# Transfers of each pair parted eight and eight over two queues, one PSUM bank, one copy and the last batch's output shares moved

## The reference

```python
def _ffn(x, w1, b1, w2, b2):
    h = gelu(x @ w1 + b1, approximate=False)          # 256 -> 1024
    return h @ w2 + b2                                # 1024 -> 256
def _attn(x, w_qkv, w_out, b_out):
    q, k, v = heads(x @ w_qkv)                        # 16 heads of 64
    sim = (q * 64 ** -0.5) @ k.T - slope_h * abs(i - j)
    sim = where(causal, -max, sim)                    # only j <= i counts
    return merge(softmax(sim) @ v) @ w_out + b_out
x = x + 0.5 * _ffn(layernorm(x), ...)
x = x + _attn(layernorm(x), ...)
x = x + 0.5 * _ffn(layernorm(x), ...)
```

## Time and profile before

| | |
|---|---|
| median of the runs | 2169.64 us |
| profiled execution | 2169.53 us |
| its span | 2167.7 us |
| PE, PEld busy | 2115.9, 1715.6 us |
| DVE, ACT, POOL busy | 1525.4, 1272.0, 1143.1 us |
| granted PE clock, mean | 0.996 of full speed |
| spread transfers | SP 1392, POOL 646, ACT 10 |

### The profile page before, as it was taken

The page is one execution under the profiler, slowest core; times in us unless marked ns, Lnnn a source line. Parts: engine busy times, 40 slices in busy tenths (PEclk is TensorE's granted clock), DMA queues, the critical chain, the costliest instruction groups (busy, mean ns, idle before and its releaser), DMA issues.

```text
span 2167.7 us, 42138 instructions
## 1 busy us (share of the span) xinstructions
PE 2115.9 (98%) x14480; PEld 1715.6 (79%) x14480; DVE 1525.4 (70%) x4121; ACT 1272.0 (59%) x3156; POOL 1143.1 (53%) x1988
## 2 busy tenths in 40 slices
PE   7999999999999999999999999999999999999998
PEld 6687787877878788787886878878787787877867
DVE  6776767767676676767767677676766777667674
ACT  5756656466565665756557465674646646565572
POOL 2754636546474563745547365473654637445361
PEclk9999999999999999999999999999999999999999
DMA  3432515234152342524425143251533415234142
GB/s 132 132 84 81 144 32 144 78 94 122 45 142 69 107 109 54 145 56 117 108 62 139 45 136 90 69 149 28 145 83 94 128 40 146 69 103 113 45 132 59
DMA packets 130294, 209.70 MB, mean 97 GB/s; under 512 B 42192, under 2 KB 70960, under 8 KB 130080
## 3 DMA queue, kind: packets, MB, share of 16 engines
q1 hardware_dynamic: 97888, 143.86, 23.6%
q0 software_dynamic: 25952, 58.38, 10.7%
q10 hardware_dynamic: 6240, 4.76, 0.8%
HBM read 14.95 MB, written 8.39 MB: 11 GB/s over the span
## 4 chain that ended last, share of the span: by engine, by line
PE 57%; DVE 19%; ACT 8%; issue 6%; POOL 4%; ACTq 3%; SPq 1%; DMA 1%; POOLq 0%; DVEq 0%
PE ps L361 56%; DVE P L937 5%; DVE gl L828 4%; ACT P L705 3%; ACTq L301 3%; DVE gh L896 2%; DVE xs L860 2%; POOL P L1126 2%; POOL PT L290 2%; DVE x L876 1%; DVE st L836 1%; SPq L290 1%; POOL rstd L1112 1%; ACT qk L651 1%; DVE xs L866 1%
## 5 line engine op out<-in xcount | busy, mean ns | idle before, releaser
L705 ACT ACTIVATE P<-P,mx 128x512 f32<-128x512 f32 (+3 forms) x1024 | 563.4, 553 | 281.6 <-DVE mx L929 281.4
L1126 POOL TENSOR_SCALAR P<-P,rs 128x512 f32<-128x512 f32 (+3 forms) x1024 | 539.2, 544 | 227.3 <-DVE rs L920 224.0
L290 POOL DMA_DIRECT2D PT<-P x646 | 324.1, 507 | 384.0 <-DVE P L937 361.1
L937 DVE STREAM_TRANSPOSE P<-P 128x1792 f32<-128x1792 f32 (+1 forms) x256 | 372.5, 1484 | 24.7 <-POOL P L1126 24.7
L361 PE MATMUL ps<-qk 64*128 64x512 f32 (+3 forms) x2048 | 321.3, 443 | 2.4 <-ACT qk L651 0.7
L361 PE MATMUL ps<-PT,v 128*64 128x256 f32 (+1 forms) x3072 | 306.7, 349 | 10.3 <-DMA PT<-P 8.7
L361 PE MATMUL ps<-w2h,gh 128*128 128x256 f32 x1024 | 291.9, 285 | 1.6 <-DVE gl L828 1.6
L361 PEld LDWEIGHTS ps<-PT,v 128*64 128x64 f32 x3072 | 204.3, 137 | 108.0 <-issue 17.1
L361 PE MATMUL ps<-w2l,gh 128*128 128x256 f32 x1024 | 289.7, 283 | 0.0
L361 PE MATMUL ps<-w2h,gl 128*128 128x256 f32 x1024 | 289.5, 283 | 0.0
L929 DVE CUSTOM_DVE_ANT_0 P<-ps,dist 128x512 f32<-128x512 f32 x256 | 166.1, 686 | 167.3 <-PE ps L361 166.8
(11 more groups left out here) (91 smaller groups left out, 4357.8 us busy)
## 6 DMA issues: line engine op xcount, KB each, us to landing
PT<-P SPq DMA_DIRECT2D x1392, 80.0 KB, 2.6
PT<-P POOLq DMA_DIRECT2D x646, 80.0 KB, 2.7
x<-in_L_attn_x SPq DMA_DIRECT2D x16, 512.0 KB, 4.4
out_y<-x SPq DMA_DIRECT2D x15, 512.0 KB, 2.9
xt<-xs SPq DMA_DIRECT2D x195, 32.0 KB, 2.0
xt<-xs POOLq DMA_DIRECT2D x165, 32.0 KB, 1.9
xt<-xs ACTq DMA_DIRECT2D x120, 32.0 KB, 2.2
raw<-in_L_ffn_w SPq DMA_DIRECT2D x2, 512.0 KB, 5.7
```

What stands on the lines that cost most here:

```text
L290: e.dma_start(PT[c % 2][32 * m:32 * m + 32, g, :], P[c % 3][32 * g:32 * g + 32, m, :]).then_inc(landed.sem, 16)
L705: e.activation(p, p, ACT.Exp, bias=mx[:, r, i:i + 1], scale=-1.0, accum_out=sm[:, r, i:i + 1]).then_inc(s_ex.sem, 1)
L937: e.transpose(p, p).then_inc(s_tr.sem, 1)
L1126: e.tensor_scalar(p, p, rs[:, 2 * (c % 2) + h, i:i + 1], 1.0, ALU.mult, ALU.mult).then_inc(s_nz.sem, 1)
```

## The change

`by_sp` now gives SP eight of the sixteen transfers and GpSimd eight; only the last two pairs of the last batch keep eleven and five (and of these SP's eleven are the six and five of SP and ScalarE). The first `dn` tile of the second feed-forward layer goes to banks 6 and 7 instead of 5. In step 6 ScalarE copies the first V tile ahead of block 2's exponentials. In the last batch the first two output shares move ahead of values(5) (and on ScalarE and VectorE ahead of the last pair's blocks), and the shares, the values and the last layernorm get other banks.

```diff
     def by_sp(pair):
-        return GROUPS[:8 if pair in pairs[:2] else 11]
+        return GROUPS[:11 if pair in pairs[-2:] else 8]
@@ begin(b), TensorE
                     up(2, b - 1, range(NM))
-                    among[0] = (5,)
+                    among[0] = (6, 7)
                     dn(2, b - 1, 0)
@@ attention(b), TensorE
-                    values(b, c - 2)
+                    if more or c < NC - 1:
+                        values(b, c - 2)
...
-                    among[0] = range(4)
-                    for c in range(4):
-                        out_part(c, range(NT))
-                    among[0] = range(4, 8)
+                    among[0] = (0, 1, 6, 7)
+                    turn[0] = 7
+                    out_part(0, range(NT))
+                    out_part(1, range(NT))
+                    among[0] = range(2, 6)
+                    values(b, NC - 3)
+                    out_part(2, range(NT))
+                    out_part(3, range(NT))
                     values(b, NC - 2)
...
-            among[0] = (6, 7)
+            among[0] = (2, 3)
             ln_transpose(3, NB - 1, 0)
@@ attention(b), ScalarE
                 for c in range(2, NC):
+                    if not more and c == NC - 1:
+                        out_part_hi(0)
+                        out_part_hi(1)
...
-                    exps(b, c, 2)
+                    if c != NC - 2:
+                        exps(b, c, 2)
                     for tile in steps_v(b, c)[:1]:
                         proj_copy(b, tile)
+                    if c == NC - 2:
+                        exps(b, c, 2)
                     exps(b, c, 0)
...
-                    for c in range(2):
+                    for c in (2, 3):
                         out_part_hi(c)
                     spread(e, b, NC - 2, LAST_ACT, s_la[NC - 2])
-                    for c in range(2, 5):
-                        out_part_hi(c)
+                    out_part_hi(4)
@@ attention(b), VectorE
                 for c in range(2, NC):
+                    if not more and c == NC - 1:
+                        out_part_lo(0)
+                        out_part_lo(1)
...
                 else:
-                    out_part_lo(0)
-                    out_part_lo(1)
+                    out_part_lo(2)
+                    out_part_lo(3)
...
-                    for c in range(2, NC):
+                    for c in range(4, NC):
                         out_part_lo(c)
```

## The result

| | before | after |
|---|---|---|
| median of the runs, on one chip | 2170.64 us (4 runs) | 2262.07 us (4 runs) |
| profiled span | 2167.7 us | 2257.1 us |
| PE busy, share | 2115.9 us, 98% | 2146.4 us, 95% |
| POOL busy | 1143.1 us | 1324.7 us |
| granted PE clock, mean | 0.996 | 0.979 |

The ratio is 1.0418, interval 1.0394 to 1.0442. Forecast were 2250 us and a range of 2205 to 2290.

What follows compares the result with a forecast made beforehand. TensorE, busy 98%, bounds the kernel, until the GpSimd and VectorE loop outgrows its step. 69.0 + 2.8 - 11.9 - 4.0 + 15.3 + 8 + 1 = 80.2 over 2169.53 us gave 2250 us, range 2205 to 2290.

Steps and rivals of the forecast that it cites:

- The loop: GpSimd and VectorE, steps 2 to 5: eight issues make each turn 9.99 us against TensorE's step of 9.05.
- values(4) later: Step 6: values(4) starts 5.75 us later in odd and 4.11 in even batches, 69.0 us in all.
- The bank: Moving down(0) off bank 5 saves 11.9 us at scores(1), but values(4) must wait for VectorE's layernorm residue.
- The clock: TensorE's idle stretches before values(4) bring half clock: 1.53 us in ten of fourteen batches, 15.3 us, bounds 0 and 21.4.
- The odd gap: Unexplained 2.5 us lost on GpSimd before pair 4's issue in seven even batches: 8 us taken, bounds 0 and 17.5.
- Batch 0: Its loop lags from pair 3 on, delaying values(4) by up to 3.2 us; 2.8 taken.
- Earlier landings: Three fewer SP issues land a pair 1.8 us sooner, saving 4.0 us of transfer waits, bounds 0 and 5.
- Last batch and tail: Last batch: the lag and moved output shares together cost 1 us, bounds -4 and +5.
- V copy: Step 6: the earlier copy ends seven waits of 1.48 us in even batches and costs nothing in odd ones.
- The first: Rival: the loop doesn't bind, only values(4)'s bank wait does, 3.0 us odd and 1.7 even: 2187 us, chance 0.08.

Runs made afterwards that it cites:

- work behind the issues: The kernel before, with four small multiplications into a spare tile on GpSimd behind each pair's five issues, no transfer moved: 2257.98 us, ratio 1.0403.
- the mended kernel: The kernel before, with down(0) on banks 6 and 7 and values(4) on the other bank than the first layernorm half: 2158.20 us, ratio 0.9937.
- The split alone: The kernel before with only the transfer split changed, to eight on SP and eight on GpSimd: 2261.32 us, ratio 1.0413.
- the other bank: The changed kernel, eight and eight kept, with values(4) on the other of banks 6 and 7: 2246.79 us, ratio 1.0353.
- waits filled: The changed kernel with useless TensorE products in the two waits of step 6, batches 1 to 14: 2247.40 us, ratio 1.0356.
- bank alone: The kernel before with only the bank of down(0) moved from 5 to 6 and 7: 2200.87 us, ratio 1.0137.
- the kernel with eleven and five: The changed kernel with the split of before, eleven transfers on SP and five on GpSimd: 2210.97 us, ratio 1.0181.
- nine and seven: The kernel before with nine transfers on SP and seven on GpSimd, last two pairs left: 2191.04 us, ratio 1.0097.
- work ahead of the issues: The changed kernel with eleven and five, plus three extra multiplications on GpSimd between normalise and each pair's issues: 2214.35 us, ratio 1.0202.
- four: The kernel before with down(0) on 6 and 7, values(4) on the other bank, twelve transfers on SP, four on GpSimd: 2165.73 us, ratio 0.9978.

## Why the prediction was right, point by point

**The loop.** Right within 0.02 us: 9.99 forecast, 10.01 measured, and shown to be the cause by the work put behind the issues.

**values(4) later.** Forecast 5.75 us in odd and 4.11 in even batches, 69.0 in all. Measured: 14.24 - 9.05 = 5.2 in odd, 14.2 - 10.97 = 3.2 in even batches inside step 6, and 0.52 more in step 5, whose stall the prediction took to be hidden behind the later bound: 5.7 and 3.8, 66 us. The order of waits was as said: 2.2 for the second half's bank, 2.5 for the residue.

**The bank.** Its gain was forecast at 11.9 and is 15 x 0.80 = 12.0; the mended kernel shows it alone. Its cost was forecast as the place at which the lag is paid. That was right for this trace, and the wrong picture of its worth. The split alone took 2261 us and the whole change 2262. With the split values(4)'s new bank costs 15 us (2262 against 2247 on the other bank), about what scores(1) gains, because the old place and the down tiles take most of the same lag. Without the split it costs 30 us by itself. The costs don't add: 91 for the split, 30 for the bank, 3 for the V copy, 0 for the last batch, and 91 for all.

**The clock.** The term that was most mis-sized: 15.3 taken, bounds 0 and 21.4. Measured in place: 25.6 us in the values rows of 14 batches. I took the price of a slow row from a wait of 2.90 us in the last batch, 1.53; behind two waits, 2.18 and 2.53, it is up to 2.16, so the upper bound itself was too low. With the waits filled the slow rows were gone, so the idle time brought them. The Trainium skill ("TensorE: Matmul & The Clock Gate", Part 1 (The HAM clock gate)) has the clock halved by default and released by activity. The trace agrees: 0.50 was granted behind the idle time, 1.00 where it was filled. But 1.0 of the 1.83 us a batch came back as another wait.

**The odd gap.** 8 taken, and no more than 1 us shows: in the changed kernel it stands ahead of the last issue of pair 5 in nearly every batch, 1.46 us, behind everything that step 6 waits for. It does delay VectorE's turn of pair 6, but TensorE's scores(7) is later still, and "later" grew by 0.07 us a batch. In the three kernels of this loop whose step 6 is shorter (split alone, other bank, waits filled) "later" is 1.0 to 2.3 us above before, and the gap, ahead of the turn of pair 6, is part of why: the kernel with work behind the issues has none there and a "later" of 50.26. Where it falls into the loop it does pass through: in the kernel with work behind the issues it is 3.4 us ahead of pair 4's issue in six of the seven even batches, and the wait before the transposes is 4.9 to 5.3 us there against 2.4 to 2.9 in the odd ones.

**The small ones.** Batch 0: 2.8 forecast, 5.4 measured. Earlier landings: 4.0 forecast, 8.7 - 6.1 = 2.6. Last batch and tail: 1 forecast, 2.7 in the trace, of which little is sure, since two traces whose last batch and split are those of before differ by 2.1 (143.0 us in the bank alone, 145.1 in the bank mended); alone its moves are 0. V copy: I priced it as a help in even batches, since the lag covers the rest; alone it is a loss of 3 us.

**Sum.** Step 6 grew by 14 x 6.04 = 84.6; 25.6 of it are the clock, which leaves 59.0, and step 5 adds 7.3. So 66.3, 25.6, 5.4 (batch 0), 0.4 (ahead of it), 2.7 (last batch and tail) and -11.2 (scores(1) in batches 1 to 14) make 89.2 of the 89.4. Against this sum the forecast of 80.2 is 9 us low. Its two largest misses nearly cancel, a clock term 10 too small and a gap term 8 too large, and that is luck. The rest is 4.0 for earlier landings, which no stage of the table shows, 2.6 for batch 0 and 2.8 for smaller terms, less 2.7 by which the delay of values(4) was too large.

**Rivals.** The first, that only the bank waits, gave the delays of the kernel with eleven and five: 3.0 in odd batches and 1.7 in even ones. Measured: 3.00, and 0.79 + 2.53 - 1.64 = 1.7. Its time, 2187, lacked the half clock (22.9 us); 2211 was measured. The Trainium skill ("DMA: Bandwidth & Descriptors", Issuing engines are not separate DMA queues) says that the sequencer's time to start a transfer, which is all that more issuing engines save, is usually small beside the transfer. Here it was the main matter: GpSimd issues for 3.98 us in a loop of 10.01. And no gain from earlier landings over 2.6 us is in the trace.

## What to carry to other kernels

Where an engine issues transfers between its arithmetic, add up the whole loop that it closes with its neighbours, wait by wait, and compare it with the bound engine's step. Past the step the excess times the number of turns arrives at the first tight wait (a loop of 8.57 us fitted under the step of 9.05 here, one of 10.01 cost 91 us in all). Look at what stands behind that wait before mending it: the mend is worth only what isn't wanted again later, 15 of the 42 us won in step 6 by the other bank. When a tile is moved in a rotation of banks, list which tile now meets which reader half a batch later: here two lines that kept that meeting apart turned a loss of 30 us into a gain of 12.

## What was not expected of the hardware

- **Which waits were followed by half clock** (values(4) rows over 2.6 us, of the waits just before them): 1.48 and 0.16 us: 0 of 7 (before); 1.44 to 1.69: 1 of 14 (nine and seven); 2.06: 1 of 7 (bank alone, odd); 1.47 and 2.35: 7 of 7 (bank alone, even); 2.17 and 0.34: 10 of 14 (other bank); 2.84: 13 of 14 (split alone); 3.00: 6 of 7 (eleven and five, odd), but 3 of 7 with work ahead of the issues; 0.79 and 2.53: 7 of 7; 2.18 and 2.53: 14 of 14 (after). The same wait was not always followed by it, and a slow row took from 2.88 to 4.54 us.
- **A gap on GpSimd that nothing in the trace releases** moves with the program: 3.14 us ahead of pair 4's issue in even batches (five issues), 1.4 to 1.6 inside pair 5's (eight), 3.4 ahead of pair 4's in six even batches (five and work behind them), 4.08 ahead of the layernorm's transfers, where it harms nothing (seven), 2.0 to 2.5 at six places (four). The number of GpSimd's instructions per batch is one thing that differs; why it comes was not tried and stays open. Inside pair 5's issues it isn't harmless: VectorE's turn of pair 6 waits 2.25 us for GpSimd with it (split alone) and 0.75 without it (work behind the issues).
